# Thirty-six weight tiles times q and k: where TensorE takes them among the query blocks and the attention blocks

## The chip, the core and the metric

The kernel runs on one core of one Trainium2 chip. The metric is the device time of one execution in microseconds (us), as the median of several runs. A smaller time is better.

## The reference, cut to what matters

1250 nodes with 768 features pass through a layer of relational graph attention (two convolutions, three relations, four heads and one head) beside a linear attention (12 heads of 64), and then through a quantised feed-forward product. The part that the change touches prepares two things of that layer: the queries of the linear attention, and, for the graph attention, the weights times the vectors q and k.

```python
xr = jnp.einsum('nd,rdf->rnf', x, W)            # graph attention, per relation r
qi = xr[etype, dst] @ q                         # so per node: x @ (W[r] @ q)
kj = xr[etype, src] @ k                         #              x @ (W[r] @ k)
alpha = jax.nn.leaky_relu(qi + kj, NEG_SLOPE)
...
qkv = x @ W_qkv + b_qkv                         # linear attention
q = where(q > 0, q + 1, exp(q))
kv = einsum('bhnd,bhne->bhde', kf, v)
y = einsum('bhnd,bhde->bhne', qf, kv) / y_den
out = y @ W_out + b_out
```

The kernel never forms q of an edge. It forms the products W[r] @ q and W[r] @ k once (768 x 8 numbers for each relation of the first convolution, 768 x 2 for the second), and multiplies the nodes by them.

## The kernel before

The program writes out one order of work for each engine by hand, and the engines meet at semaphores. The stage of interest lies between the sums of the linear attention's keys and values (line 1867) and the output product (line 1995). Three kinds of TensorE work are woven together there.

**Query products.** The queries of 1280 padded nodes are computed in six query blocks of 128 features, q = 3 * c + fb. A block is six steps (k = 0 to 5, one for each 128 rows of the weights), and a step is 12 fp16 matmuls with 320 columns, line 1911: three splits of high and low parts times four groups of nodes. At the end of the sixth step DVE adds the bias (line 1451) and with ScalarE forms phi of the four groups (lines 994, 996 and 1456), two groups at a time. The first step of the next block waits at line 1910 (`q_free`) until DVE has read the banks.

**Count windows.** The graph's edges are turned into a count matrix, one window of 21 destination nodes after the other. For each window DVE builds one-hot rows of at least seven tiles of 125 edges (`oh_q` line 1345, `oh_p` line 1346), and `count_window` multiplies them on TensorE (line 1824, two matmuls of 315 columns for each tile; four tiles first, then groups of three in a loop) and ends with one small matmul (line 1839). ScalarE copies the counts out (line 956), SyncE stores them (line 477). There is one set of seven one-hot slots, so DVE can build window w + 1 only as TensorE consumes window w. A query block has three windows, `wa`, `wa + 1` and `wa + 2`: before step 2, before step 4, and after step 5. One more window (`W_A - 1`) follows the sixth block. In DVE's order the rows of the next block's first window come directly after the four groups' phi. In the second half (c = 1), three additions to X (line 1461) come right behind them.

**Weight tiles.** There are 36 tiles, 18 for each convolution. `wq_tile(t)` (lines 1873 to 1887) takes one 128 x 768 fp32 tile of the transposed weights as six stationary blocks, each multiplied by 8 columns (`qkn`) or 2 (`qkn2`), into PSUM banks 4 and 5. In the trace such an fp32 matmul is two instructions, so a tile is 12 of them (line 1885). The tiles live in three buffers `wt`; `wq_load(t)` on SyncE (line 627) loads tile t once tile t - 3 has been used. ScalarE and DVE read the banks only after all 36.

**Where the tiles stand.** The table `Q_TILES = (0, 3, 8, 13, 18, 22, 26)` gives query blocks 0 to 5 their 3, 5, 5, 5, 4 and 4 tiles, and `step_tile` puts each of them singly ahead of a step: steps 3 to 5 in block 0, steps 1 to 5 in blocks 1 to 3, steps 2 to 5 in blocks 4 and 5. The remaining ten stand in the ten attention blocks, one in each.

**Attention blocks.** For each 128 nodes i, TensorE transposes the normalised result of block i (line 1936), multiplies the queries of block i + 1 (`weighted`, line 1925), takes a count window (blocks 0 to 7) and then a tile. DVE normalises block i + 1 (lines 1468 to 1477), forms the low part of block i (line 1490), and builds the one-hot rows of the next window. The output product begins when all ten blocks are through.

Of the kernel before, what the change touches and what calls it, by code (L numbers as in the profile page):

```python
# [31 lines left out]
K6 = D // P  # L32
# [35 lines left out]
WT_TILES = 2 * R * K6  # L68
# [18 lines left out]
def build(nc, x, src, dst, et, W1, q1, k1, b1, W2, q2, k2, b2, Wqkv, bqkv, Wo, bo, wf, bf, W1t, W2t, out):  # L87
    ctx = ExitStack()
    with ctx:
        def sem(name):  # L90
            return ctx.enter_context(nc.semaphore(name))
# [13 lines left out]
        def place(name, shape, dt, offset):  # L105
            return nc.alloc_sbuf_tensor_at(name, shape, dt, offset=base + KEEP + -(-offset // 32) * 32)
# [68 lines left out]
        cc_ = [place(f"cc{j}", [P, QN], U16, 145408 + 1280 * j) for j in range(2)]  # L175
# [133 lines left out]
        kvd_done = sem("kvd_done")  # L309
# [17 lines left out]
        qkn_in = sem("qkn_in")  # L327
# [118 lines left out]
        def window(eng, w):  # L446

            word = eng.value_load(tabrow[0:1, ds(w, 1)], min_val=0, max_val=(NWN * MAXG << 16) + (MAXG << 9) + NT)
            tile0 = eng.snap(word & 511, min_val=0, max_val=NT - 1)
            count = eng.snap((word >> 9) & 127, min_val=1, max_val=MAXG)  # L450
            first = eng.snap(word >> 16, min_val=0, max_val=NWN * MAXG)
            return tile0, count, first

        W_K, W_V, W_S, W_Q = 0, NB, 3 * NB, 3 * NB + 3
        W_A = W_Q + 3 * K6 + 1

        Q_TILES = (0, 3, 8, 13, 18, 22, 26)

        def block_windows(i):

            return range(W_A + i, min(W_A + i + 1, NWN))

        def block_tiles(i):

            return range(Q_TILES[-1] + i, Q_TILES[-1] + i + 1)

        def step_tile(q, k):

            t = Q_TILES[q + 1] - K6 + k
            return range(t, t + 1) if t >= Q_TILES[q] else range(0)  # L470

        assert W_A + NB >= NWN and block_tiles(NB - 1)[-1] == WT_TILES - 1

        def store_window(sp, w, stage, u):

            sp.wait_ge(ct_ev, w + 2)
            sp.dma_start(ct_d[:, ds(w, 1), :].rearrange("p o n -> p (o n)"), stage[u][:, :]).then_inc(ct_out[u], 16)
# [92 lines left out]
        def _(sp):  # L570
# [52 lines left out]
            def wq_load(t):  # L623
                if t >= 3:
                    sp.wait_ge(wt_used, t - 2)
                w = (W1t, W2t)[t // (WT_TILES // 2)]
                sp.dma_start(wt[t % 3][:, :], w[t // K6 % R, t % K6 * P:(t % K6 + 1) * P, :]).then_inc(wt_in[t % 3], 16)
# [2 lines left out]
                wq_load(t)  # L630
            chunk_load(7)
            for q in range(K6):
                for k in range(1, K6):
                    if k in (3, 5):
                        store_window(sp, W_Q + 3 * q + k // 2 - 1, cc_, (3 * q + k // 2 - 1) % 2)
                    for t in step_tile(q, k):
                        wq_load(t + 3)
                store_window(sp, W_Q + 3 * q + 2, cc_, (3 * q + 2) % 2)
            store_window(sp, W_A - 1, cc_, (W_A - 1 - W_Q) % 2)
            for i in range(NB):  # L640
                sp.wait_ge(xb_done, i + 2)
                sp.dma_start(acc_d[i * P:(i + 1) * P, :], X[:, i, :]).then_inc(xs_out, 16)
                for w in block_windows(i):
                    store_window(sp, w, cc_, (w - W_Q) % 2)
                for t in block_tiles(i):
                    if t + 3 < WT_TILES:
                        wq_load(t + 3)
# [75 lines left out]
            for h in range(H):  # L723
# [3 lines left out]
                for r in range(R):  # L727
                    i = h * R + r
# [1046 lines left out]
        def _(pe):  # L1775
# [20 lines left out]
            with pe.Fori(0, NB // 2) as ii:  # L1796
                for j in range(2):
                    i = 2 * ii + j
# [19 lines left out]
            def count_window(w, bank, count, first):  # L1818

                pe.wait_ge(ct_ev, w + 1)  # L1820

                def tile(u, start):
                    for q in range(2):
                        last = pe.matmul(ps[:, bank + q, 0:QH], oh_p[0:ET, u, :], oh_q[0:ET, u, q * QH:(q + 1) * QH],  # L1824
                                         start=start, stop=False, skip_group_check=True)
                    return last

                for i in range(2):
                    pe.wait_ge(oh_rdy[i], w + 1)
                    for u in range(2 * i, 2 * i + 2):  # L1830
                        last = tile(u, u == 0)
                    last.then_inc(oh_free[i], 1)
                with pe.Fori(0, count) as jj:
                    n1 = pe.snap(first + jj + 1)
                    pe.wait_ge(oh_rdy[2], n1)
                    for u in range(TF, TG):
                        last = tile(u, False)
                    last.then_inc(oh_free[2], 1)
                pe.matmul(ps[:, bank + 1, 0:2], ident16[:, :], zrow[:, 0:2], start=False, stop=True, skip_group_check=True).then_inc(ct_cnt, 1)
# [34 lines left out]
            def wq_tile(t):  # L1874

                r, nb = t // K6 % R, t % K6
                pe.wait_ge(wt_in[t % 3], 16 * (t // 3 + 1))
                for k in range(K6):
                    if t < WT_TILES // 2:
                        o = ps[:, 4, k * 2 * R * H:(k + 1) * 2 * R * H].rearrange("p (t x) -> p t x", t=2)[:, :, r * H:(r + 1) * H]  # L1880
                        q = qkn[:, nb, :, :]
                    else:
                        o = ps[:, 5, k * 2 * R:(k + 1) * 2 * R].rearrange("p (t x) -> p t x", t=2)[:, :, r]
                        q = qkn2[:, nb, :]
                    last = pe.matmul(o, wt[t % 3][:, k * P:(k + 1) * P], q, start=(t % (WT_TILES // 2) == 0 and k == 0), stop=(nb == K6 - 1),  # L1885
                                     skip_group_check=True)
                last.then_inc(wt_used, 1)
# [3 lines left out]
            for c in range(2):  # L1891
                cc = C_Q + c
                pe.wait_ge(w_lo_done, cc + 1)
                for fb in range(3):
                    wa = W_Q + 3 * (3 * c + fb)
                    of_w = [window(pe, wa + u)[1:] for u in range(3)]
                    for k in range(K6):
                        if k in (2, 4):
                            count_window(wa + k // 2 - 1, 6, *of_w[k // 2 - 1])
                        for t in step_tile(3 * c + fb, k):  # L1900
                            if t == 0:
                                pe.wait_ge(kvd_done, 2)
                                pe.wait_ge(qkn_in, 64)
                            wq_tile(t)
                        w_h, w_l = w_hi[cc % 2][:, k, fb * P:(fb + 1) * P], w_lo[cc % 2][:, k, fb * P:(fb + 1) * P]
                        for step, (w, t) in enumerate(((w_h, xt_hi), (w_h, xt_lo), (w_l, xt_hi))):
                            for g in range(NRG):
                                n = (3 * c + fb) * NRG + g
                                if k == 0 and step == 0:
                                    pe.wait_ge(q_free, n + 1)  # L1910
                                last = pe.matmul(ps[:, g, 0:RG], w, t[:, k, g * RG:(g + 1) * RG], start=(k == 0 and step == 0),  # L1911
                                                 stop=(k == K6 - 1 and step == 2))
                                if k == K6 - 1 and step == 2:
                                    last.then_inc(q_done, 1)
                    count_window(wa + 2, 6, *of_w[2])

            of_w = window(pe, W_A - 1)[1:]
            count_window(W_A - 1, 6, *of_w)
            pe.wait_ge(q_out, 2 * 3 * NRG + 2)
            def weighted(i):  # L1920
# [9 lines left out]
            for i in range(NB):  # L1930
                pe.wait_ge(y_n, i + 1)
                for hf in range(2):
                    if i >= 1:
                        pe.wait_ge(y_lo, 2 * i - 1 + hf)
                    for k in range(3):
                        last = pe.transpose(ps[:, 2 + hf, k * P:(k + 1) * P], yn[i % 2][:, (3 * hf + k) * P:(3 * hf + k + 1) * P], ident[:, :])
                    last.then_inc(y_tr, 1)
                if i + 1 < NB:
                    weighted(i + 1)
                for w in block_windows(i):  # L1940
                    count_window(w, 6, *window(pe, w)[1:])
                for t in block_tiles(i):
                    wq_tile(t)
# [255 lines left out]
```

## Time and profile before

| | before |
|---|---|
| runs, median (lowest to highest) | 1757.9 us (1757.42 to 1764.39), 3 runs |
| profiled execution, its own time | 1760.24 us |
| profiled execution, span from first to last instruction | 1758.5 us |
| TensorE (PE) busy | 1621.5 us, 92% of the span |
| VectorE (DVE) busy | 1308.4 us, 74% |
| ScalarE (ACT) busy | 774.4 us, 44% |
| mean granted TensorE clock | 0.966 of 2.4 GHz |

The page's slices and the views of the trace give times in us from the start of the span. Line numbers are those of the printed kernel. A busy share of an engine says nothing of whether that engine holds the end: for that, the view of the chain that ended last follows the work back from the end to what released each step.

### The profile page before, as it was taken

How to read it: one execution, taken by the hardware profiler on the slowest of the kernel's cores; microseconds unless marked ns; L12 is line 12 of the kernel's file. 1: busy time of each engine (PE TensorE's matmuls, PEld its weight loads, DVE VectorE, ACT ScalarE, POOL GpSimd, SP SyncE). 2: the span in 40 equal slices, each digit the busy share in tenths (PEclk: the TensorE clock that was granted, in tenths of full speed). 3: DMA queues.
4: the chain of work that ended last, by engine and by line, in shares of the span. 5: the costliest groups of instructions: out<-in, count | busy, mean ns of one | idle time of the engine just before them, and what ended most of it. 6: DMA issues, size and time to landing. Idle time of an engine off the chain costs nothing.

```text
span 1758.5 us, 34402 instructions
## 1 busy us (share of the span) xinstructions
PE 1621.5 (92%) x10547; PEld 1179.7 (67%) x10548; DVE 1308.4 (74%) x2631; ACT 774.4 (44%) x1021; POOL 138.1 (8%) x245
## 2 busy tenths in 40 slices
PE   4999999987999999889999999989889799999987
PEld 3566667766755666469999999986555455555544
DVE  8698875578749999248899898973664377777785
ACT  4331112222234555168888898863211133333342
POOL 2000000000000000000000000000000033333340
PEclk8999999999899999989999999989999999999999
DMA  5111133323557664541003132132654541011212
GB/s 197 32 58 59 61 73 117 102 79 98 163 157 236 195 194 150 154 128 59 30 30 116 61 110 61 51 98 79 196 171 150 182 154 53 1 53 53 65 55 88
DMA packets 130308, 183.30 MB, mean 104 GB/s; under 512 B 14934, under 2 KB 100088, under 8 KB 130220
## 3 DMA queue, kind: packets, MB, share of 16 engines
q1 hardware_dynamic: 130220, 182.17, 33.4%
q8 instruction: 49, 0.80, 0.2%
q14 instruction: 39, 0.32, 0.1%
HBM read 121.33 MB, written 60.81 MB: 104 GB/s over the span
## 4 chain that ended last, share of the span: by engine, by line
PE 75%; DVE 10%; issue 5%; DMA 3%; ACT 3%; DVEq 2%; POOL 1%; SPq 1%; ACTq 0%; POOLq 0%
PE ps L2044 22%; PE ps L1995 12%; PE ps L2102 7%; PE ps L2101 7%; PE ps L1811 5%; PE ps L1813 4%; PE ps L1812 4%; PE ps L1824 4%; PE ps L1911 2%; PE ps L1885 2%; DVE oh_q L1345 2%; DVE oh_p L1346 1%; PE ps L2113 1%; PE ps L1980 1%; DMA xr_d<-ev 1%
## 5 line engine op out<-in xcount | busy, mean ns | idle before, releaser
L2044 PE MATMUL ps<-xrh,pf 128*128 (+1 forms) x2400 | 399.9, 329 | 11.3 <-DVE pf L1622 11.3
L2044 PEld LDWEIGHTS ps<-xrh,pf 128*128 128x128 f32 x2400 | 393.5, 191 | 17.8 <-issue 15.4
L1811 PE MATMUL ps<-w_hi,xt_hi 128*128 128x384 f16 x600 | 199.6, 333 | 23.9 <-DVE ev L1668 15.4
L1345 DVE TENSOR_SCALAR oh_q<-pat,codeT,neg_w 125x630 f16<-125x630 uint16 x420 | 185.8, 442 | 41.3 <-PE ps L1824 29.7
L1618 DVE SCALAR_TENSOR_TENSOR vb<-vb,tb 128x1260 f32<-128x1260 f32 x120 | 172.9, 1467 | 54.7 <-ACT vb L1119 53.8
L2101 PE MATMUL ps<-x,ph 128*128 (+1 forms) x600 | 196.5, 327 | 16.8 <-POOL pl L921 10.8
L1622 DVE SCALAR_TENSOR_TENSOR pf<-vb,CT 128x1260 f32<-128x1260 f32 x120 | 175.8, 1468 | 35.3 <-PE ps L2044 35.3
L1812 PE MATMUL ps<-w_lo,xt_hi 128*128 128x384 f16 x600 | 199.2, 332 | 0.0
L1813 PE MATMUL ps<-w_hi,xt_lo 128*128 128x384 f16 x600 | 199.1, 332 | 0.0
L2102 PE MATMUL ps<-x,ph 128*128 (+1 forms) x600 | 197.9, 330 | 0.0
L1119 ACT ACTIVATE vb<-qbc,kcol 128x1260 f32<-128x1260 f32 x120 | 161.0, 1345 | 39.5 <-DVE pf L1622 38.1
L1529 DVE CUSTOM_DVE_ANT_0 tt_junk<-kbc,mb 126x1260 bf16<-126x1260 f32 x120 | 169.1, 1466 | 10.0 <-issue 10.0
L1114 ACT ACTIVATE tb<-qbc,kcol_leak 128x1260 f32<-128x1260 f32 x120 | 159.6, 1343 | 20.2 <-DVE vb L1618 18.9
L1824 PE MATMUL ps<-oh_q,oh_p 125*128 125x315 f16 x840 | 132.1, 304 | 23.7 <-DVE oh_p L1346 23.1
L1181 ACT ACTIVATE ph<-p 128x252 f16<-128x252 f32 x150 | 61.9, 413 | 161.5 <-PE ps L2102 158.5
L921 POOL TENSOR_TENSOR pl<-p,ph 128x252 f16<-128x252 f32 x150 | 111.1, 742 | 197.4 <-ACT ph L1181 186.0
L1995 PE MATMUL ps<-w_hi,xt_hi 128*128 128x384 f16 x360 | 118.9, 330 | 7.4 <-ACT ev L1043 7.4
L1824 PEld LDWEIGHTS ps<-oh_q,oh_p 125*128 125x128 f16 x840 | 80.9, 99 | 66.3 <-DVE oh_p L1346 20.1
L1995 PE MATMUL ps<-w_lo,xt_hi 128*128 128x384 f16 x360 | 118.7, 330 | 0.0
L1995 PE MATMUL ps<-w_hi,xt_lo 128*128 128x384 f16 x360 | 118.5, 329 | 0.0
L1668 DVE TENSOR_TENSOR ev<-ps,ev 128x384 f16<-128x384 f32 x60 | 32.8, 556 | 101.1 <-ACT ev L1168 97.9
L1811 PEld LDWEIGHTS ps<-w_hi,xt_hi 128*128 (+1 forms) x600 | 59.7, 99 | 68.7 <-issue 32.4
(235 smaller groups left out, 2451.1 us busy)
## 6 DMA issues: line engine op xcount, KB each, us to landing
qbc<-tq_d SPq DMA_DIRECT2D x12, 1260.0 KB, 6.6
wst<-in_L_gnn_W SPq DMA_DIRECT2D x60, 192.0 KB, 3.2
xr_d<-ev SPq DMA_DIRECT2D x60, 192.0 KB, 2.0
xrh<-xr_d SPq DMA_DIRECT2D x4, 2880.0 KB, 14.8
x_d<-ev SPq DMA_DIRECT2D x60, 192.0 KB, 2.3
mb_d<-mb SPq DMA_DIRECT2D x30, 310.1 KB
mb<-mb_d SPq DMA_DIRECT2D x30, 310.1 KB
x<-x_d SPq DMA_DIRECT2D x2, 3840.0 KB, 18.9
```

The lines of the kernel that those rows point to most:

```text
L1345: dve.tensor_scalar(oh_q[0:ET, u, :], pat[0:ET, :], codes[:, k:k + 1], neg_w[0:ET, ds(w, 1)], ALU.subtract, ALU.is_equal)
L1529: dve.tensor_tensor_reduce(out=tt_junk[k][0:WK, :], in0=kbc[0:WK, h, :], in1=mb[w % 2][0:WK, :], scale=1.0, scalar=2 * BIG, op0=ALU.subtra ...
L1618: dve.scalar_tensor_tensor(vb[j][:, :], vb[j][:, :], 2.0, tb[j][:, :], ALU.min, ALU.max).then_inc(v_step, 1)
L1622: dve.scalar_tensor_tensor(pf[j][:, 0:ND].rearrange("p (w d) -> p w d", d=WN), vb[j][:, :].rearrange("p (w d) -> p w d", d=WN), 2.0, CT[:, ...
L1811: pe.matmul(ps[:, bank, 0:CW], a_hi, hi[:, k, :], start=(k == 0), stop=False)
L1812: pe.matmul(ps[:, bank, 0:CW], a_hi, lo[:, k, :], start=False, stop=False)
L1813: last = pe.matmul(ps[:, bank, 0:CW], a_lo, hi[:, k, :], start=False, stop=(k == K6 - 1))
L1824: last = pe.matmul(ps[:, bank + q, 0:QH], oh_p[0:ET, u, :], oh_q[0:ET, u, q * QH:(q + 1) * QH], start=start, stop=False, skip_group_check= ...
L1995: mm = pe.matmul(ps[:, 6 + n % 2, 0:CW], a[:, k, i * P:(i + 1) * P], w[:, k, :], start=(q % PM == 0), stop=(q % PM == PM - 1))
L2044: mm = pe.matmul(out[b], pf[j][:, b * DB:b * DB + P], x, start=(first and b % 2 == 0), stop=False, skip_group_check=True)
L2101: pe.matmul(ps[:, bank, 0:CW], p, cols(off, off + CW), start=start, stop=False, skip_group_check=True)
L2102: mm = pe.matmul(ps[:, bank + 1, 0:CW + n1], p, cols(off + CW, off + D + n1), start=start, stop=False, skip_group_check=True)
```

## The change

The same 36 tiles are taken, in the same order, in other places. Query block q takes three tiles in a row (3q to 3q + 2) after its sixth step and ahead of its third count window. The next three (18 to 20) stand in a row ahead of the window `W_A - 1`. The first five attention blocks take two tiles each (21 to 30) and the last five one each. SyncE's order of loads and stores follows: in a query block it first issues the stores of two windows, then the loads of the three tiles that follow next, then the third store. The wait for the constants of the first tile (`kvd_done`, `qkn_in`) moves with it.

```diff
-        Q_TILES = (0, 3, 8, 13, 18, 22, 26)
 ...
         def block_tiles(i):
-            return range(Q_TILES[-1] + i, Q_TILES[-1] + i + 1)
-
-        def step_tile(q, k):
-            t = Q_TILES[q + 1] - K6 + k
-            return range(t, t + 1) if t >= Q_TILES[q] else range(0)
+            t = WT_TILES // 2 + 3
+            return range(t + 2 * i, t + 2 * i + 2) if i < 5 else range(t + 5 + i, t + 6 + i)
 ...
@@ SyncE @@
             for q in range(K6):
-                for k in range(1, K6):
-                    if k in (3, 5):
-                        store_window(sp, W_Q + 3 * q + k // 2 - 1, cc_, (3 * q + k // 2 - 1) % 2)
-                    for t in step_tile(q, k):
-                        wq_load(t + 3)
+                for u in range(2):
+                    store_window(sp, W_Q + 3 * q + u, cc_, (3 * q + u) % 2)
+                for t in range(3 * q + 3, 3 * q + 6):
+                    wq_load(t)
                 store_window(sp, W_Q + 3 * q + 2, cc_, (3 * q + 2) % 2)
+            for t in range(WT_TILES // 2 + 3, WT_TILES // 2 + 6):
+                wq_load(t)
             store_window(sp, W_A - 1, cc_, (W_A - 1 - W_Q) % 2)
 ...
@@ TensorE @@
                         if k in (2, 4):
                             count_window(wa + k // 2 - 1, 6, *of_w[k // 2 - 1])
-                        for t in step_tile(3 * c + fb, k):
-                            if t == 0:
-                                pe.wait_ge(kvd_done, 2)
-                                pe.wait_ge(qkn_in, 64)
-                            wq_tile(t)
 ...
+                    if c == 0 and fb == 0:
+                        pe.wait_ge(kvd_done, 2)
+                        pe.wait_ge(qkn_in, 64)
+                    for t in range(3 * (3 * c + fb), 3 * (3 * c + fb) + 3):
+                        wq_tile(t)
                     count_window(wa + 2, 6, *of_w[2])
 
             of_w = window(pe, W_A - 1)[1:]
+            for t in range(WT_TILES // 2, WT_TILES // 2 + 3):
+                wq_tile(t)
             count_window(W_A - 1, 6, *of_w)
```

## Rows read from the trace of the kernel before

**Rows 1.** The page: busy time by engine, and the last chain by engine.
```profile
PE 1621.5 (92%) x10547; PEld 1179.7 (67%) x10548; DVE 1308.4 (74%) x2631; ACT 774.4 (44%) x1021; POOL 138.1 (8%) x245
...
PE 75%; DVE 10%; issue 5%; DMA 3%; ACT 3%; DVEq 2%; POOL 1%; SPq 1%; ACTq 0%; POOLq 0%
```

**Rows 2.** Busy us (x instructions) by stretch: PE, PEld, DVE, ACT, POOL, clock, DMA, GB/s.
```profile
277.10:303.00 25.90, 23.30 (x182) 17.58 (x180) 15.45 (x52) 5.94 (x12) 0.00 (x0) 1.00 0.33 96
...
415.00:475.00 60.00, 52.70 (x422) 46.04 (x422) 56.68 (x187) 15.28 (x31) 2.20 (x9) 0.96 0.45 137
```

**Rows 3.** Last chain in query blocks 1 and 2: start, us, what.
```profile
286.82 1.35 PE ps L1885 x12
288.17 1.65 PE ps L1911 x12
289.81 1.24 PE ps L1885 x12
...
292.70 1.91 PE ps L1824 x14
...
298.84 1.39 PE ps L1911 x10
300.23 0.55 DVE q_t L1451
...
310.66 0.99 PE ps L1824 x6
...
313.01 3.21 PE ps L1911 x12
```

**Rows 4.** Timeline of PE, start of query block 1, idle before in brackets.
```profile
278.69 0.77 PE L1911 MATMUL ps<-xt_hi,w_hi 128*128 128x320 f16 x2 [1.09 <-DVE q_t L1451]
...
285.82 0.99 PE L1824 MATMUL ps<-oh_q,oh_p 125*128 125x315 f16 x6 [0.83 <-DVE oh_p L1346]
```

**Rows 5.** Last chain: a tile of block 0, ends of blocks 0 and 5.
```profile
264.27 1.68 PE ps L1885 x12
...
275.13 0.55 DVE q_t L1451
...
402.66 0.55 DVE q_t L1451
```

**Rows 6.** Timeline of DVE, end of block 3 to block 4's second window.
```profile
351.53 1.01 DVE L1451 TENSOR_SCALAR q_t<-ps,bq_col 128x320 f32<-128x320 f32 x2 [3.03 <-PE ps L1911]
...
361.73 2.69 DVE L1461 TENSOR_TENSOR X<-X,bsum 128x768 f32 x3
...
367.79 0.24 DVE L1346 TENSOR_SCALAR oh_p<-iota_l,sloT 125x128 f16<-125x128 f16 x1
```

**Rows 7.** Timeline behind block 5: window W_A - 1, first normalisation.
```profile
410.47 2.26 PE L1824 MATMUL ps<-oh_q,oh_p 125*128 125x315 f16 x8 [5.64 <-DVE oh_p L1346]
...
416.54 0.23 DVE L1468 TENSOR_SCALAR rdn<-ps 128x6 f32<-128x6 f32 x2 [0.16 <-PE ps L1925]
```

**Rows 8.** Timeline of PE, one attention block and the start of the next.
```profile
424.20 0.85 PE L1936 MATMUL ps<-ident,yn 128*128 128x128 f32 x6
...
428.01 0.99 PE L1824 MATMUL ps<-oh_q,oh_p 125*128 125x315 f16 x6 [0.52 <-DVE oh_p L1346]
...
428.87 1.48 PE L1885 MATMUL ps<-qkn,wt 128*128 128x2 f32 x12
430.20 0.85 PE L1936 MATMUL ps<-ident,yn 128*128 128x128 f32 x6
```

**Rows 9.** The loads of tile wt, from issue to landing.
```profile
DMA to landing us min/median/max: 2.8/3.4/7.4
```

**Rows 10.** Stretches around two falls of the clock, columns as in rows 2.
```profile
308.00:312.00 4.00, 3.13 (x24) 1.97 (x22) 3.89 (x16) 0.28 (x1) 0.00 (x0) 1.00 0.30 95
312.00:316.00 4.00, 4.00 (x21) 2.73 (x22) 2.42 (x10) 0.42 (x1) 0.00 (x0) 0.61 0.47 130
...
440.00:444.00 4.00, 3.97 (x29) 3.75 (x30) 3.93 (x14) 1.68 (x3) 0.00 (x0) 0.82 0.41 88
```

## The prediction, made before the changed kernel ran

> **What bounds the kernel now.** I read the page first. TensorE is busy 92% of the span and holds 75% of the last chain [rows 1], but the shares say nothing of this stage. So I read the stage by its stretches: a query block takes 25.9 us with DVE busy for only 15.5 of them, while the attention blocks keep DVE busy for 56.7 of 60 us [rows 2]. The first stage has room for more work beside other work, the second has little. Which part of a query block has that room is told by the chain of waits [rows 3]. It has two halves.
>
> Half A runs from the bias addition after the sixth step (300.23) to the end of the next block's first window (310.66 + 0.99 = 311.65), 11.4 us. It runs over DVE and ScalarE: four groups of phi, then the one-hot rows. TensorE has only the third window, two steps, a tile and the first window to do in it, and waits 1.09 us for the banks and 0.83 us for the rows [rows 4].
>
> Half B runs from there (286.82) to the next bias addition (300.23), 13.4 us. It is TensorE without a pause: four tiles (1.35, 1.24, and two more like them, 5.2 us), four steps (three of 1.65 and the chain's 1.39 of the last) and a window of 1.91. Every tile in half B is paid in full.
>
> **The change in the query blocks.** Half B loses its tiles: 13.4 - 5.2 = 8.2 us. Half A gains tiles. From the bias addition TensorE has 0.1 us of the sixth step left, then three tiles (1.34 + 1.24 + 1.24 = 3.8), the third window (1.9), two steps (3.3) and the first eight of the next window's fourteen matmuls (8/14 of 1.91, 1.1): 10.2 us. The last of those one-hot rows comes 10.4 us after the bias addition (300.23 to 310.66 [rows 3]). So the three tiles fit into half A with 0.2 us to spare. DVE takes 3.6 us for seven one-hot rows (361.73 + 2.69 = 364.4 to 368.0 [rows 6]), so it asks for free slots only 10.4 - 3.6 = 6.8 us after the bias addition, when the third window has ended (5.8 us), so the delayed window hurts nobody. A block then takes 11.42 + 8.25 = 19.7, or 19.9 for block 1, whose half A is 11.7 (275.13 to 286.82 [rows 3, 5]).
>
> In blocks 4 and 5 something else is late next. The additions to X stand between the rows of the first and second window. They begin at 361.73, and the second window's last row is ready at 367.79 + 0.24 = 368.0, which is 16.5 us after the bias addition at 351.53 [rows 6]. In the new order TensorE would like it at 15.7 (half A of 11.3, two steps of 1.65, eight matmuls of 1.1). I add 0.8 to 0.9: 20.4 us for these two.
>
> The end of block 0 is at 275.13, that of block 5 at 402.66 [rows 5]: 127.5 us for five blocks. After: 19.9 + 2 x 19.7 + 2 x 20.4 = 100.1, a gain of 27.4. Block 0 loses three tiles of 1.68, 1.34 and 1.24 [rows 5, 3] from its chain, but the step behind the first then runs 0.4 us longer in a stretch of slow clock: a gain of 3.9. Sum -31.3 us. Eight tiles leave these blocks; the rest of the gain is waits that are filled.
>
> **Behind block 5.** TensorE now stands idle 5.64 us before the window W_A - 1, and the first normalisation starts at 416.54, 13.9 us after block 5's bias addition [rows 5, 7]; DVE's additions hold it as much as TensorE (0.16 us of waiting). After: 0.1, three tiles 3.8, window 1.9, three tiles 3.8, window 1.9, weighted 1.4 (in rows 8 it lies between the transposes and the window), together 12.9. So at full clock it costs nothing, with a cover of 1.0 us.
>
> **The attention blocks.** A block takes 6.0 us (424.20 to 430.20) with 0.52 us of waiting for DVE [rows 8]. A second tile adds 1.25: five give 6.25, less 5 x 0.52 = 2.6 of waits that they fill, 3.7 us on TensorE. DVE sets the pace here. The product of the next block is ready when the window begins (428.01 - 0.52 - 1.1 = 426.4), and DVE turns to it after the one-hot rows, at about 428.0: 1.6 us of cover. So its lag is 3.7 - 1.6 = +2.1 us. The later blocks do not give that back, since DVE is full.
>
> **SyncE and DMA.** The three loads of a group go out as each of the three tiles is used, and the next group is needed a whole block later; a load lands in 3.4 us, at worst 7.4 [rows 9]. The shortest distance is in the attention blocks and behind block 5, about 4.5 to 6.5 us. I cost it at nothing; without that cover, at worst 1 to 3 us in each such place. The stores of the windows keep their place relative to the windows.
>
> **The clock is the term of unknown size.** A tile's matmuls have 8 or 2 columns. In the trace the clock falls to 1.2 GHz at 312.9 after a stretch in which TensorE was busy 3.13 of 4 us, but with one tile and waits in it, and again at 442.6, after 3.97 of 4 busy us, where a tile stood beside a wait [rows 10]. Busy time did not hold it. I therefore count tile time as idle time for the clock. The price of a fall: the first step behind it took 3.21 us in place of 1.65 [rows 3], so 1.6 us. A row of three tiles, 3.8 us, is longer than what stood before either fall, so I expect one fall in nearly every block, in half A where the cover is small: 1.6 - 0.2 = 1.4 us in each of blocks 1 to 3 and about 0.5 in 4 and 5, which wait for DVE anyhow; with a second fall in one block it is +6.0 in sum (bounds: 0; two falls in every block, 3 x 3.0 + 2 x 2.1 = 13.2). Before had two such falls (the last of rows 3 in block 2, and one more like it in block 4), which are in the 127.5. Behind block 5 six tiles stand close: two falls, 3.2 less the cover of 1.0, +2.2 (0 to 4.0). In the attention blocks I take two falls in the five with two tiles, +3.2 (0 to 6.4), since each row is only 2.6 us.
>
> The Trainium skill ("TensorE: Matmul & The Clock Gate", Part 1) says that the throttled state is the default and that activity releases it, and Part 4 that work in transpose mode does not count as busy in the same way. By busy time alone there would be no fall at tiles and the sum would be -29.2; with tiles as idle it is the sum below. The rows speak for the second.
>
> **The sum.** -31.3 + 6.0 (clock) + 2.2 (behind block 5, clock) + 2.1 + 3.2 (attention, clock) = -17.8 us. The profiled execution took 1760.24 us (the span of 1758.5 and 1.7 around it), so 1742.4; it stands 2.3 us above the median of the runs, so against 1757.9 I forecast 1740.1 us. Bounds: no falls -29.2 (1728.7); all of them -31.3 + 13.2 + 4.0 + 8.5 = -5.6 (1752.3).
>
> **The rivals.**
> 1. The clock eats the gain: two falls in every block and the upper bounds elsewhere, 1752. For it: tiles stood before both falls. Against: full steps follow the tiles, and in block 2 the clock was back within the 4 us in which it fell (mean 0.61 [rows 10]).
> 2. Slower: the clock stays at 1.2 GHz over most of each query block, because each row of tiles, stretched to twice its time, brings the next fall. The block has 19 us of TensorE work, and each us at half clock loses 0.5. It decides from 12.5 us of slow clock per block on: 6.25 lost x 5 = 31.3, which takes up the -31.3; with 4.0 and 8.5 behind it, about 1770.
> 3. The tiles were covered anyway: DVE sets the block's length as in the attention stage. Then only the eight tiles that leave the blocks count, 8 x 1.29 = 10.3, and 5 x 1.25 = 6.3 comes back in the attention blocks: -4.0, 1753.9. Against: DVE waits for TensorE in half B and is busy 15.5 of 25.9 us [rows 2].
> 4. Transfers come late: two tiles and X's block for each attention block, landing at the worst value, 1 us in each of five blocks: 1745.5.
>
> **Chances.** Forecast 0.72, rival 1 0.10, rival 2 0.07, rival 3 0.07, rival 4 0.04. A measurement tells about 0.5% from no change, 8.8 us, so faster is below 1749.1. Forecast and rival 4 are faster (0.76), rivals 1 and 3 the same (0.17), rival 2 slower (0.07). The range holds all but rival 2 and the far ends: 1730 to 1755.
>
> **What would show it.** Right: no TensorE wait at the first step of a block, blocks 19.7 to 21.5 us apart by their bias additions, one slow stretch behind each row of three tiles, the 5.64 us wait gone, attention blocks of 6.6 us or more while they take two tiles, and waits of TensorE for `wt` absent. Wrong: blocks still 25 us long (rival 3), a granted clock near half over whole blocks (rival 2), TensorE waiting for loads of `wt` (rival 4), or a slot or store that a later window holds up.

## The result: 1746.4 us against 1758.7 us, and the profile after

| | before | changed |
|---|---|---|
| median of the runs (lowest to highest) | 1758.66 us (1756.38 to 1764.39), 6 runs | 1746.43 us (1742.97 to 1753.14), 6 runs |
| ratio, 95% interval | | 0.9929 [0.9906, 0.9952] |
| profiled execution, own time | 1760.24 us | 1746.55 us |
| its span | 1758.5 us | 1744.8 us |
| mean granted clock | 0.966 | 0.962 |

The change makes the kernel 12.2 us (0.7%) faster. The forecast was 1740.1 us, 17.8 us under the profiled execution's own time: the direction is right, the measured time lies in the range, and the gain is about two thirds of what was forecast. Line numbers in the views are those of the kernel that is shown, so one piece of work has several: a tile is L1885 in the kernel before and L1880, L1890 or L1891 elsewhere, a count window L1824, L1819 or L1826, a step L1911, L1901, L1913 or L1914. The page of the changed kernel, against rows 1:

```profile
PE 1631.8 (94%) x10547; PEld 1191.5 (68%) x10548; DVE 1308.5 (75%) x2631; ACT 774.8 (44%) x1021; POOL 138.1 (8%) x245
...
PE 80%; DVE 8%; issue 4%; DMA 3%; ACT 2%; DVEq 1%; POOL 1%; SPq 1%; ACTq 0%; POOLq 0%
```

The same 10547 matmul instructions take 10.3 us more busy time, and the kernel is still shorter. The chain has moved from DVE (10% to 8%) to TensorE (75% to 80%): waits were filled, and TensorE itself ran slower in places. Cut at the marks that the prediction used, the spans of the two traces are these:

| stretch | before | changed | forecast for the change | measured |
|---|---|---|---|---|
| up to the bias addition of block 0 | 275.1 | 271.1 | -3.9 | -4.0 |
| five query blocks | 127.5 | 109.1 | -27.4, clock +6.0 | -18.4 |
| behind block 5, to the first normalisation | 13.9 | 18.5 | +2.2 | +4.6 |
| from there to the output product | 58.1 | 66.7 | +2.1, clock +3.2 | +8.6 |
| all that follows, not touched | 1283.9 | 1279.4 | 0 | -4.5 |

The last chain through a query block of the changed kernel (start, us, what), against rows 3:

```profile
292.52 4.56 PE ps L1880 x36
297.08 3.70 PE ps L1819 x14
...
300.79 4.14 PE ps L1901 x24
304.92 1.91 PE ps L1819 x14
...
306.84 3.28 PE ps L1901 x24
310.12 1.91 PE ps L1819 x14
...
312.04 3.28 PE ps L1901 x24
```

There is no DVE in it. The bias addition has left the chain, the wait for the banks and that for the one-hot rows [rows 4] are gone, and three tiles (x36) stand where the chain ran over phi. Half B is nearly what was forecast: 3.28, 1.91, 3.28 and no tile, 8.5 us against 8.2. But the row of tiles takes 4.56 us in place of the 3.8 that the prediction took, the same 14 matmuls of a window take 3.70 us behind it and 1.91 us elsewhere, and the next two steps 4.14 in place of 3.28. That is the clock. The granted clock is either 2.4 or 1.2 GHz (1.00 in most stretches of 4 us of the kernel before, 0.50 from 260 to 264 us), so a mean of 0.85 says that it was at 1.2 GHz for about three tenths of the stretch. The stretches of the changed kernel (columns as in rows 2): two query blocks, the part behind block 5, the attention blocks, and the rest.

```profile
271.20:292.40 21.20, 21.20 (x157) 15.88 (x155) 15.06 (x51) 5.62 (x11) 0.00 (x0) 0.92 0.26 80
292.40:315.20 22.80, 22.80 (x156) 16.91 (x155) 15.08 (x51) 5.62 (x11) 0.00 (x0) 0.85 0.24 74
...
380.30:398.70 18.40, 18.33 (x116) 15.09 (x114) 11.00 (x27) 6.94 (x11) 0.00 (x0) 0.72 0.52 154
398.70:465.40 66.70, 62.49 (x469) 56.35 (x470) 55.26 (x184) 14.89 (x30) 2.20 (x9) 0.88 0.50 149
465.40:1744.80 1279.40, 1208.28 (x7689) 883.70 (x7689) 939.67 (x1455) 652.31 (x819) 119.99 (x183) 0.97 0.35 109
```

TensorE is busy for all of a block. At a mean clock of 0.92 the block takes 21.2 us, at 0.85 it takes 22.8. The changed kernel's five blocks come in these two sizes: 21.2, 22.8, 21.2, 21.2 and 22.8 us. In the two longer ones the clock fell earlier in the row of tiles, and the row itself took 4.73 and 5.00 us in the timeline, against 4.08 to 4.37 in the other three.

### The profile page after: what moved, and what is told of

The parts are those of the page before. It is cut to its first block, busy times and chain, and to the rows that moved or that the text cites. A ratio compares the mean times of both kernels' runs of the same rounds, so it can differ in the third digit from the quotient of the medians.

```text
span 1744.8 us, 34402 instructions
## 1 busy us (share of the span) xinstructions
PE 1631.8 (94%) x10547; PEld 1191.5 (68%) x10548; DVE 1308.5 (75%) x2631; ACT 774.8 (44%) x1021; POOL 138.1 (8%) x245
## 4 chain that ended last, share of the span: by engine, by line
PE 80%; DVE 8%; issue 4%; DMA 3%; ACT 2%; DVEq 1%; POOL 1%; SPq 1%; ACTq 0%; POOLq 0%
PE ps L2041 22%; PE ps L1992 12%; PE ps L2099 7%; PE ps L2098 7%; PE ps L1819 6%; PE ps L1806 4%; PE ps L1807 4%; PE ps L1808 4%; PE ps L1901 3%; PE ps L1880 3%; PE ps L2110 1%; PE ps L1977 1%; DVE oh_q L1340 1%; DMA xr_d<-ev 1%; PE ps L1862 1%
## 5 line engine op out<-in xcount | busy, mean ns | idle before, releaser
L1340 DVE TENSOR_SCALAR oh_q<-pat,codeT,neg_w 125x630 f16<-125x630 uint16 x420 | 186.4, 444 | 34.3 <-PE ps L1819 23.5
L1109 ACT ACTIVATE tb<-qbc,kcol_leak 128x1260 f32<-128x1260 f32 x120 | 159.6, 1343 | 20.2 <-DVE vb L1613 18.8
L1819 PE MATMUL ps<-oh_q,oh_p 125*128 125x315 f16 x840 | 140.6, 322 | 9.0 <-DVE oh_p L1341 8.5
L1819 PEld LDWEIGHTS ps<-oh_q,oh_p 125*128 125x128 f16 x840 | 87.4, 106 | 52.3 <-DVE oh_p L1341 7.1
```

The source lines that it names most:

```text
L1340: dve.tensor_scalar(oh_q[0:ET, u, :], pat[0:ET, :], codes[:, k:k + 1], neg_w[0:ET, ds(w, 1)], ALU.subtract, ALU.is_equal)
```

## Experiments

The kernels below keep the 36 tiles in their order. Most change only how many tiles stand at each place. A query block has eight places: ahead of steps 0 to 5, ahead of the third window (place 6) and behind it (place 7). The loads and stores on SyncE follow TensorE's order. Ratios are against runs of the kernel before on the same chip.

### Three tiles for each block, but not next to each other

```diff
-query blocks 0 to 5: place 6: 3
+block 0: places 6, 7: 1 each; blocks 1 to 4: places 1, 6, 7: 1 each; block 5: place 1: 1, place 6: 3
```

The first kernel also splits the pairs of the first five attention blocks:

```diff
-attention blocks 0 to 4: behind the window: 2
+attention blocks 0 to 4: ahead of the window: 1, behind it: 1
```

> Counts as in the changed kernel (18 tiles in the query blocks, three ahead of window W_A - 1, two in each of the first five attention blocks), but hardly any tile stands next to another: in query blocks 0 to 4 one ahead of the third window, one behind it, one ahead of step 1 of the next block; in the attention blocks one ahead of and one behind the window. Only block 5's end and the window W_A - 1 keep rows of three. Theory (waits are filled, rows of tiles make the clock fall): query blocks 19.7 to 20.4 us apart with no slow stretch, attention 58 to 60 us from the first transpose to the output product in place of 65.1, so about 14 us faster than the changed kernel: 1732. Rival (the rows do not matter, TensorE's total work sets the time): within 2 us of the changed kernel, 1746.

Measured: 1731.6 us (1729.2 to 1735.5, 6 runs), ratio 0.9832 [0.98, 0.9864]. The second kernel has the query blocks alone split:

> As e2_all_singly in the query blocks, as the changed kernel in the attention blocks (pairs). Theory: the query blocks give 9 us over the changed kernel (99.9 in place of 109.1 us over five blocks), the attention blocks stay at about 65 us: 1737. The difference to e2_all_singly, 5 us, is then the price of the pairs. Rival (rows do not matter): 1746, as e2_all_singly.

Measured: 1739.5 us (1735.4 to 1741.2, 6 runs), ratio 0.9872 [0.984, 0.9904]. Two blocks without additions to X, one with them, and the attention blocks of the first kernel (columns as in rows 2):

```profile
270.30:290.20 19.90, 19.61 (x155) 15.06 (x154) 15.02 (x51) 5.51 (x11) 0.00 (x0) 1.00 0.27 85
290.20:309.80 19.60, 19.60 (x155) 15.10 (x154) 14.98 (x51) 5.51 (x11) 0.00 (x0) 1.00 0.28 86
329.50:350.10 20.60, 19.77 (x156) 14.93 (x155) 17.48 (x54) 5.51 (x11) 0.00 (x0) 1.00 0.25 82
390.70:449.90 59.20, 55.28 (x469) 50.38 (x470) 55.20 (x184) 14.69 (x30) 2.20 (x9) 0.98 0.56 171
```

The same work, at the same counts, takes 19.6 to 20.6 us for a block with a granted clock of 1.00. The rows of three were what brought the clock down, and without them the five blocks take 100.3 us in both kernels, in place of 109.1. In block 4 TensorE waits for DVE's one-hot rows at the second window, as the prediction's step on the additions to X had it (timeline of TensorE):

```profile
345.96 0.99 PE L1826 MATMUL ps<-oh_q,oh_p 125*128 125x315 f16 x6 [0.83 <-DVE oh_p L1348]
```

The rival that rows do not matter is out. The two kernels differ by the pairs alone: 7.9 us of the medians, where 5 were expected. The traces show 2.8 us of it in the attention blocks (59.2 against 62.1) and 4.1 in the rest, where the kernels do not differ.

### The pairs alone

```diff
-attention blocks 0 to 4: behind the window: 2
+attention blocks 0 to 4: ahead of the window: 1, behind it: 1
```

> The changed kernel, but the pairs of the first five attention blocks are split: one tile ahead of the window, one behind it. Theory: no slow stretch inside the attention blocks, 59 to 60 us from first normalisation to output product in place of 62 to 67, so 3 to 7 us under the changed kernel: 1740 to 1743. Rival (pairs cost nothing beyond their work): 1746.

Measured: 1742.5 us (1737.6 to 1744.7, 6 runs), ratio 0.9892 [0.9857, 0.9926]. The query blocks keep their rows of three and repeat the changed kernel's 21.2, 22.8, 21.2, 21.2, 22.8. The attention blocks:

```profile
398.50:457.80 59.30, 54.75 (x469) 49.84 (x470) 55.18 (x184) 14.69 (x30) 2.20 (x9) 0.98 0.55 168
```

59.3 us at a clock of 0.98, in place of 66.7 at 0.88. So the five extra tiles cost 1.2 us over the 58.1 of before when they stand singly, and up to 8.6 in pairs. What the pairs cost differs between traces: in the kernel with only the query blocks split the same pairs took 62.1 us, and in the kernel of the next section but one 62.0. The difference is how often the clock fell. In the changed kernel three stretches of 12 us have low means:

```profile
400.00:412.00 12.00, 11.42 (x82) 10.02 (x83) 10.86 (x41) 2.44 (x5) 0.00 (x0) 0.86 0.38 105
412.00:424.00 12.00, 12.00 (x97) 11.13 (x96) 10.90 (x38) 2.50 (x5) 0.00 (x0) 0.91 0.57 169
424.00:436.00 12.00, 12.00 (x71) 10.88 (x70) 6.09 (x22) 2.42 (x5) 0.00 (x0) 0.66 0.51 134
```

In the kernel with only the query blocks split, the four such stretches from 391 us on have means of 0.86, 1.00, 1.00 and 1.00.

### The same counts as before, in one row

```diff
-query blocks, singly ahead of steps 1 to 5: 3, 5, 5, 5, 4, 4
+query blocks, place 6: 3, 5, 5, 5, 4, 4
```

> Counts as in the kernel before (3, 5, 5, 5, 4, 4 in the query blocks, one in each attention block), but in one row behind the sixth step of each block, ahead of the third window. Theory: the row is longer (6.3 us) than the cover, and part of it runs at the slow clock: blocks 2 to 5 at 23.5 to 25.5 us, block 1 at 21.2, so 5 to 10 us faster than before: 1748 to 1753, with two slow stretches in most blocks. If the clock played no part, TensorE's work alone would give 21.7 us for a block: 1735. Rival (place within the block does not matter, only the count): as before, 1758.

Measured: 1753.9 us (1752.0 to 1757.9, 12 runs), ratio 0.9958 [0.9937, 0.9978]. The gain over before is real, but the blocks are longer than the expected 23.5 to 25.5: 21.2, 27.1, 27.2, 27.2 and 24.3 us, and the time is at the far end of the expected 1748 to 1753. A block with a row of five, and the row itself in the timeline of TensorE:

```profile
291.70:318.80 27.10, 27.10 (x179) 21.74 (x177) 15.12 (x50) 5.62 (x11) 0.00 (x0) 0.81 0.31 92
```

```profile
291.84 9.89 PE L1890 MATMUL ps<-qkn,wt 128*128 128x8 f32 x60
```

Five tiles at 1.25 would be 6.3 us. They took 9.9, since much of the row itself ran at the low clock, and the window behind it took 3.83. TensorE's work alone is 21.7 us by the expectation's sum, and about 22.1 by the split kernel's 19.6 and two tiles more, so the clock takes 5.0 to 5.4 us of each such block. Every wait of before is filled here, and yet blocks 2 to 4 are longer than before's 24.8 to 26.5 us. The gain in this stage lies in blocks 0 and 1; behind block 5 it loses 2.1 us (16.0 against 13.9).

### The same counts as the changed kernel, ahead of steps 3, 4 and 5

```diff
-query blocks, place 6: 3
+query blocks, places 3, 4, 5: 1 each
```

> Counts as in the changed kernel everywhere, the tiles behind block 5 and in the attention blocks in the changed kernel's rows and pairs, but in the query blocks singly ahead of steps 3, 4 and 5, where TensorE is the chain. Theory: nothing is filled in half A, blocks take 11.4 + 12.1 = 23.5 us, the rows behind block 5 and the pairs cost as in the changed kernel: slower than the changed kernel by 10 to 15 us, 1757 to 1762. Rival (the gain is the eight tiles that left the query blocks, wherever the rest stand): as the changed kernel, 1746.

Measured: 1756.2 us (1751.6 to 1764.6, 12 runs), ratio 0.9976 [0.9955, 0.9998], just under the 1757 to 1762 expected and hardly to be told from before. A block, and the part behind block 5:

```profile
323.40:346.90 23.50, 20.31 (x155) 14.84 (x154) 15.02 (x51) 7.53 (x12) 0.00 (x0) 1.00 0.24 71
395.30:409.30 14.00, 12.21 (x81) 9.36 (x78) 11.09 (x27) 6.83 (x11) 0.00 (x0) 0.76 0.39 126
```

The blocks without a fall take the 23.5 us of the working, at full clock and with the waits of half A still open (TensorE is busy 20.3 of 23.5 us). The five blocks take 120.8 us with two falls among them. The eight tiles that left the query blocks thus give 6.7 us there (127.5 before), and 3.9 comes back in the attention blocks (62.0 against 58.1). That is not the changed kernel's gain of 18.4 in the blocks: the rest of it comes from waits that the tiles fill. The second row shows that three tiles ahead of window W_A - 1, with none ahead of the window before it, cost nothing: 14.0 us against 13.9. (The mean clock of 0.76 there is no loss against before, which has 0.75 in the same stretch.)

### Columns into the row

One matmul of 384 columns ahead of each of a tile's six fp32 matmuls, into unused columns of bank 5; otherwise the changed kernel.

```diff
                 for k in range(K6):
+                    pe.matmul(ps[:, 5, P:P + CW], xt_hi[:, k, 0:P], xt_hi[:, k, 0:CW], start=False, stop=False, skip_group_check=True)
                     last = pe.matmul(o, wt[t % 3][:, k * P:(k + 1) * P], q, ...)
```

> The changed kernel's order with one 384-column fp16 matmul added ahead of each of a tile's six fp32 matmuls, into unused columns of bank 5. It is a look at the clock, not a faster kernel. Theory (a row of tiles counts as idle because its matmuls have 8 or 2 columns): with columns in the row the clock stays at 2.4 GHz in the query blocks, all five blocks take the same time, and the extra matmuls cost their stream of at most 6 x 0.16 = 1.0 us for a tile: blocks of up to 19.5 + 2.9 = 22.4 us. Rival (the clock falls for another reason, such as fp32 weights or the order): slow stretches stay in every block and the blocks take 24 us or more. Total about 1755 to 1765 by the theory, since 18 tiles outside the query blocks get longer too.

Measured: 1744.0 us in one run. One run makes no comparison of times, but the trace says what the kernel was made for. Two query blocks, the part behind block 5, and the attention blocks:

```profile
271.50:292.50 21.00, 21.00 (x173) 16.62 (x171) 15.01 (x51) 5.63 (x11) 0.00 (x0) 1.00 0.26 80
292.50:313.50 21.00, 21.00 (x173) 16.61 (x171) 15.03 (x51) 5.64 (x11) 0.00 (x0) 1.00 0.25 81
...
376.50:392.80 16.30, 16.30 (x152) 15.00 (x150) 11.03 (x26) 6.95 (x11) 0.00 (x0) 1.00 0.55 156
392.85:458.70 65.85, 62.05 (x558) 57.09 (x558) 55.42 (x184) 14.69 (x30) 2.21 (x9) 1.00 0.51 155
```

All five blocks take 21.0 us at full clock, and the six tiles behind block 5 and the pairs in the attention blocks run at full clock too. The order, the rows and the fp32 weights are the changed kernel's; only the wide matmuls were added, and the falls in all these stretches are gone. The Trainium skill ("TensorE: Matmul & The Clock Gate", Part 1) says that activity releases the throttle; these rows agree, if a row of narrow matmuls, busy in every record, is taken as too little activity, as the prediction took it.

The added matmul differs from the tile's in two ways, in its columns and in its type (fp16 beside fp32). The changed kernel's own trace speaks against the type. Far behind the stage, fp32 matmuls with many columns (line 2041, 193 where the trace gives the form) are all that TensorE does for 50 us, and the clock stays full. And 180 fp16 matmuls with 6 columns in a row (lines 1948 to 1950, from 1179.90 to 1184.7 us) are followed by a fall while the row runs. The third line is the four us around that fall:

```profile
1100.00:1150.00 50.00, 49.99 (x304) 49.25 (x303) 45.42 (x38) 44.80 (x37) 0.00 (x0) 1.00 0.04 12
1179.90:1183.10 3.20, 3.20 (x127) 3.20 (x128) 1.92 (x1) 1.25 (x1) 0.00 (x0) 0.99 0.00 0
1183.00:1187.00 4.00, 3.69 (x73) 2.83 (x71) 0.96 (x2) 0.71 (x2) 0.00 (x0) 0.51 0.01 4
```

That row comes after a wait of 1.29 us, so it is a sign and not a test. No kernel here gives the tiles more fp16 matmuls without more columns.

The added work is nearly free. A tile takes 1.80 us in place of 1.25, so the wide matmuls add 0.55 us and not the 1.0 that their streams alone would cost, and the block is not longer than the changed kernel's shortest. That, and the falls saved, puts the one time under the expected 1755 to 1765.

### The part behind block 5

The kernel with everything split, but block 5 takes one tile (ahead of step 1), three stand ahead of W_A - 1, and three more go to attention blocks 5 to 7.

```diff
-block 5: place 1: 1, place 6: 3; attention blocks 0 to 4: 1 ahead, 1 behind
+block 5: place 1: 1;             attention blocks 0 to 7: 1 ahead, 1 behind
```

> As e2_all_singly, but behind block 5's sixth step stands no tile, three stand ahead of window W_A - 1, and the other three are in attention blocks 5 to 7 (two in each of blocks 0 to 7, one ahead of and one behind the window). Theory (the six tiles behind block 5 cost 6 us, mostly at the slow clock, while three fit into the idle time, as in e5_three_in_steps): from the last bias addition of block 5 to the first normalisation 14 us in place of 20.1, attention 1 to 2 us longer: 1727. Rival (the stretch behind block 5 is slow whatever stands in it, because TensorE idles there): 1732 or more.

Measured: 1729.8 us (1726.8 to 1732.2, 6 runs), ratio 0.982 [0.9787, 0.9853]. The part behind block 5 with six tiles (first line, the kernel with everything split) and with three (second line, this one):

```profile
370.60:390.70 20.10, 20.00 (x116) 17.25 (x114) 11.09 (x27) 6.94 (x11) 0.00 (x0) 0.66 0.41 130
```

```profile
369.50:384.10 14.60, 12.70 (x81) 9.84 (x78) 11.09 (x27) 6.83 (x11) 0.00 (x0) 0.77 0.35 114
```

The other three tiles of the six cost 5.5 us there, at a mean clock of 0.66. Three alone cost 0.6 us over before's 13.9. The same six tiles in the same two rows took 18.5 us in the changed kernel and 20.1 here, so this price, too, depends on where the falls come. The three that moved cost 3.1 us in the attention blocks (62.3 us), more than the 1 to 2 expected, so 2.4 us is left by the traces and 1.8 by the medians, which is inside the scatter of the runs.

The last kernel takes the three additions to X apart:

> As e7_tail_of_three, with DVE's three additions to X taken apart: in blocks 3 to 5 one stands behind each of the three count windows' one-hot rows in place of three behind the last. Theory (in blocks 4 and 5 these additions make the second window late, and behind block 5 they hold the first normalisation): blocks 4 and 5 at 19.7 in place of 20.6 us and up to 2 us less behind block 5: 3 us under e7_tail_of_three, 1724. Rival (DVE is full there and only the place of the delay changes): as e7_tail_of_three, 1727.

```diff
                     for u in range(2):
                         count_part(W_Q + 3 * (3 * c + fb) + u + 1)
+                        if c == 1:
+                            dve.tensor_tensor(sub(X, 3 * fb + u), sub(X, 3 * fb + u), bsum[:, :], ALU.add).then_inc(xb_done, 1)
...
-                        for u in range(3):
+                        for u in range(2, 3):
```

Measured: 1728.8 us (1727.3 to 1731.0, 6 runs), ratio 0.9822 [0.9789, 0.9855]: not to be told from the last. Blocks 4 and 5 fell from 20.6 to 20.2 and 20.0 us, but block 3 rose from 19.6 to 20.0, and the part behind block 5 gave 0.7. That is 1.3 us in the traces where 3 were expected. The additions did hold blocks 4 and 5, but block 3 takes 0.4 of their 0.9 us back. DVE is busy for 17.5 of the 20.2 us of block 4, which may be why not more was gained; no run tests it.

## Why the prediction came out as it did

**The two halves of a block: right.** The working gave 19.9, 19.7, 19.7, 20.4 and 20.4 us for the blocks at full clock. The kernel with the tiles split measured 19.9, 19.65, 19.6, 20.6 and 20.6: it has the same three tiles in the same half, though not all in the changed kernel's places. So 27.2 us of the 27.4 are there when the clock holds. The step on block 0 (-3.9) measured -4.0, with luck in the closeness: in the eight traces without a tile ahead of this mark it comes at 269.2 to 271.4 us, which is 3.7 to 5.9 earlier than before. The rival that the tiles were covered anyway fell with the run of three tiles ahead of the steps. It also gave 1753.9 us, outside the measured interval. The rival of late loads fell with the trace: no matmul on a tile waited in the changed kernel. (The kernel with the tiles ahead of steps 3 to 5 has one such wait, 1.04 us at its first tile.) The loads of tile wt in the changed kernel, against rows 9:

```profile
DMA to landing us min/median/max: 2.8/3.7/8.2
```

**The clock: right in kind, too small in size.** The term that was mis-sized in the query blocks is "one fall in nearly every block, a second in one": every row of three brought a slow stretch, and in two of five blocks a double one. So two blocks were 22.8 us apart, outside the 19.7 to 21.5 that the prediction named as its sign. Against the split kernel the rows cost 109.1 - 100.3 = 8.8 us in place of 6.0. The price of a fall was right: a single stretch costs 1.3 to 1.5 us in blocks 1 and 3 and a double one 3.2 in block 2. In blocks 4 and 5 the cover from the additions to X saved about 0.8 us, where 0.9 was taken (21.2 and 22.8 against 20.6). But the sum had a slip: three times 1.4, twice 0.5 and 1.6 for the second fall are 6.8 and not 6.0, so of the 2.8 us that were missing, 0.8 are the slip, and most of the other 2.0 is the second double stretch.

One reading of the rows was also wrong. The prediction has the clock back within the 4 us in which it fell in block 2 (mean 0.61). A clock at half from 312.9 to the end of that stretch gives this same mean, and the step at 1.2 GHz lasts until 313.01 + 3.21 = 316.2 [rows 3]. The prediction used this row only against its first rival. (By rival 4's own terms its time is 1745.1, not 1745.5.)

**Behind block 5: mis-sized.** +2.2 was forecast, +4.6 measured. At full clock the work fits, as the run with added columns shows: its 16.4 us between the marks less 6 x 0.55 of added work are 13.1, where 12.9 was worked out. But with six tiles close together the clock was low for over half of the stretch (mean 0.72). The stretch of before has a similar mean, 0.75, yet there TensorE was idle for 5.9 of the 13.8 us, and here it works through all of it. A tile that runs at the low clock takes twice its time (three took 7.82 us in the split kernel there, against 4.08 in block 3 of the changed one) and so makes the row longer. I had counted falls at a fixed price of 1.6 us.

**The attention blocks: mis-sized in this trace.** The work of five more tiles was put at +2.1, and the tiles measured +1.2 when they stand singly. That number is not the work alone, since before's mean clock was 0.96 there and the split kernel's 0.98. The clock was put at +3.2. It took 7.4 us in the changed kernel's trace (66.7 against 59.3), but 2.8 in the two other kernels with pairs (62.1 and 62.0), so in those the term was about right. By the medians the pairs cost 4.0 us in one comparison, whose runs were not taken together (6.5 by their ratios to before), and 7.9 in the other. I took a pair, 2.6 us, to be too short to bring a fall each time, and indeed not every pair does. Here is one that did, in the timeline of TensorE: the transposes and the weighted product take 0.85 and 1.51 us in one attention block, and 1.52 and 2.81 behind the pair that follows.

```profile
415.73 0.85 PE L1933 MATMUL ps<-ident,yn 128*128 128x128 f32 x6
416.42 1.51 PE L1922 MATMUL ps<-kvd,QF 128*128 128x130 f32 x12
...
419.70 3.28 PE L1880 MATMUL ps<-qkn,wt 128*128 128x2 f32 x24
422.85 1.52 PE L1933 MATMUL ps<-ident,yn 128*128 128x128 f32 x6
424.16 2.81 PE L1922 MATMUL ps<-kvd,QF 128*128 128x130 f32 x12
```

**The sum.** In the profiled pair the touched stretches gave 9.2 us where 17.8 were forecast: 2.9 us short in the query blocks (with block 0), 2.4 behind block 5, 3.3 in attention. Another 4.5 us of the difference of the spans lie in the rest, which no edit touches. Over the ten traces of this case that rest took 1279.4 to 1284.0 us, so a part of this size comes and goes by itself. So the median's 12.2 us owes something to luck: with the touched stretches alone the gain would be about 9. What makes the rest vary was not settled; the traces show slow stretches of the clock there at changing places.

The rival "the clock eats the gain" was thus half true. The prediction gave it 0.10 as a case of its own, and it would have been better told as the upper half of the forecast. The slower rival, that the rows of tiles feed the low clock, did not decide here, but its mechanism shows in part: with rows of five the clock took 5.0 to 5.4 us of a block, and blocks 2 to 4 became longer than before. It stopped short of the slow clock over most of a block that the rival needs (mean 0.81).

## What to carry to other kernels

Work that moves off the chain into an engine's waits is worth what the two halves of the loop say. At full clock this could be worked out from the trace before to a few tenths of a microsecond for each block. But ask what the filler does to TensorE's clock. Rows of matmuls with few columns were followed by falls here. The same matmuls standing singly were not, in the split kernels' query blocks, though before had two falls where single tiles stood beside waits. So spread them between dense matmuls and do not gather them. The kernel took 1759 us with most tiles singly in the half that TensorE bounds, 1746 with rows in the other half, and about 1730 with them singly in that other half.

## What the runs showed that was not expected

A matmul of 384 columns, 0.16 us long by itself, added 0.09 us to each fp32 matmul with 8 columns (a tile 1.80 us in place of 1.25). That could mean that such tiles are held by loading their weights, beside which columns are cheap, but no run takes this apart. A kernel with 216 more matmuls ran once in 1744.0 us, where the one without them took 1743.0 to 1753.1.

A row of five tiles is not 5/3 of a row of three: 9.9 us against 4.1 to 5.0. The clock falls while the row still runs, and the rest of the row is stretched.
